# Graph layer kernel on one core: the second kind's tiles one lot earlier, and mask and maximum in one operation

## The reference, cut to what matters

```
h = relu(layernorm(x))
feat = concat(h[src], h[dst])
e_f  = relu(feat @ W_kind + b_kind)            # kind by the edge's number: 128 hh, 640 oo, 7680 ho
logit = e_f @ W_a + b_a
m = segment_max(logit, dst);  ex = exp(logit - m[dst])
alpha = ex / segment_sum(ex, dst)[dst]
z = segment_sum(alpha * h[src], dst)
x = x + relu(concat(h, z) @ (W_hn for nodes 0..63, W_on for 64..255) + b)
h = relu(layernorm(x));   W = zeros(1024, 1024); W[src, dst] += edge_weight
out = x + h @ W.T + bias
```

## Time and profile before

| | |
|---|---|
| median of 3 runs | 334.21 us (333.5 to 334.31) |
| the profiled execution's own time | 336.71 us |
| its span | 334.9 us |
| PE busy | 307.4 us (92%) |
| DVE busy | 255.0 us (76%) |
| ACT busy | 176.8 us (53%) |
| POOL busy | 159.2 us (48%) |
| DMA moved | 122.06 MB, mean 364 GB/s |
| granted TensorE clock | 0.99 of full |

### The profile page before, as it was taken

How to read it: one execution, slowest core, us unless ns; L and a number is a source line. 1 busy time by engine, 2 the same in 40 slices (tenths; PEclk the granted TensorE clock), 3 DMA queues, 4 the chain that set the end, 5 groups by cost and what they waited for, 6 DMA issues and landing times.

```text
span 334.9 us, 4146 instructions
## 1 busy us (share of the span) xinstructions
PE 307.4 (92%) x1363; PEld 195.8 (58%) x1363; DVE 255.0 (76%) x433; ACT 176.8 (53%) x437; POOL 159.2 (48%) x148
## 2 busy tenths in 40 slices
PE   0899999999999899999999999959998998889995
PEld 0687688745657466556666665645733554533533
DVE  4645527465999998998688888599897969996244
ACT  3865342371467663878356566466534847652102
POOL 3030057306877778788458887567777300000000
PEclk9999999999999999999999999979999999999997
DMA  7999979999999999999999999999999999999003
GB/s 247 409 410 410 363 247 297 373 415 339 352 394 410 410 409 409 410 407 412 415 410 410 409 411 411 414 410 409 410 408 412 406 410 406 405 408 350 17 0 125
DMA packets 34425, 122.06 MB, mean 364 GB/s; under 512 B 4058, under 2 KB 4570, under 8 KB 34404
## 3 DMA queue, kind: packets, MB, share of 16 engines
q0 software_dynamic: 19008, 69.21, 52.7%
q1 hardware_dynamic: 14004, 47.34, 36.7%
q10 hardware_dynamic: 1392, 5.24, 3.8%
HBM read 115.49 MB, written 6.29 MB: 364 GB/s over the span
## 4 chain that ended last, share of the span: by engine, by line
PE 29%; POOL 25%; DMA 25%; DVE 10%; issue 8%; ACT 2%; ACTq 0%; DVEq 0%
DMA Gq<-q_ho,ids 24%; POOL Gq L383 13%; PE psG L850 13%; POOL Gp L369 12%; PE psG L961 5%; DVE Gp L668 3%; PE psG L1063 2%; DVE Gp L672 2%; PE psG L1058 1%; PE psG L1014 1%; DMA xs<-x 1%; PE psW L1052 1%; PE psW L900 1%; ACT h L404 1%; DVE Wl L621 1%
## 5 line engine op out<-in xcount | busy, mean ns | idle before, releaser
L668 DVE TENSOR_TENSOR Gp<-Gp,Gq 128x1024 f32<-128x1024 f32 x65 | 79.4, 1221 | 26.2 <-DMA Gq<-q_ho,ids 24.1
L383 POOL DMA_INDIRECT Gq<-q_ho,ids x60 | 74.0, 1233 | 45.4 <-DVE Gp L668 16.1
L369 POOL DMA_INDIRECT Gp<-p_ho,ids x60 | 67.8, 1129 | 44.3 <-DMA p_ho<-T 24.4
L992 PE MATMUL psG<-W,hT 128*128 128x512 f32 x192 | 85.3, 594 | 0.0
L672 DVE SCALAR_TENSOR_TENSOR Gp<-Gp,wa 128x1024 f32<-128x1024 f32 x65 | 79.0, 1216 | 0.3
L478 ACT ACTIVATE RW<-ohs,ewh 128x256 fp32r<-128x256 f32 x66 | 33.2, 504 | 58.6 <-DVE ohs L659 54.3
L992 PEld LDWEIGHTS psG<-W,hT 128*128 128x128 f32 x192 | 35.6, 191 | 39.3 <-issue 38.9
L900 PE MATMUL psW<-RW,ohd 128*128 128x256 f32 x264 | 44.7, 291 | 0.4
L900 PE MATMUL psA<-RL,ohd 128*128 128x256 f32 x240 | 37.4, 299 | 8.1 <-ACT RL L488 7.4
L900 PEld LDWEIGHTS psA<-RL,ohd 128*128 128x128 f32 x240 | 31.7, 195 | 14.0 <-ACT RL L488 13.5
L900 PEld LDWEIGHTS psW<-RW,ohd 128*128 128x128 f32 x264 | 36.3, 189 | 4.1 <-issue 2.9
(11 more groups left out here) (174 smaller groups left out, 356.9 us busy)
## 6 DMA issues: line engine op xcount, KB each, us to landing
W<-weights SPq DMA_DIRECT2D x63, 512.0 KB, 7.4
Gp<-weights SPq DMA_DIRECT2D x8, 512.0 KB, 9.8
Gq<-weights SPq DMA_DIRECT2D x4, 512.0 KB, 12.6
pre_f<-weights SPq DMA_DIRECT2D x3, 512.0 KB, 7.3
xs<-x SPq DMA_DIRECT2D x2, 512.0 KB, 3.9
h_rows<-h ACTq DMA_DIRECT2D x1, 1024.0 KB, 6.7
pre_l<-weights SPq DMA_DIRECT2D x2, 512.0 KB, 7.0
p_ho<-T ACTq DMA_DIRECT2D x2, 512.0 KB, 5.0
```

The costliest lines, as they stand in the source:

```text
L369: nc.gpsimd.indirect_dma_start(out=Gp[:, i % NP, :], out_offset=None, in_=p_oo if t <= OO_TILES else p_ho, in_offset=bass.IndirectOffsetOn ...
L383: nc.gpsimd.indirect_dma_start(out=Gq[:, i % NQ, :], out_offset=None, in_=q_oo if t <= OO_TILES else q_ho, in_offset=bass.IndirectOffsetOn ...
L668: nc.vector.tensor_tensor(Gp[:, i % NP, :], Gp[:, i % NP, :], Gq[:, i % NQ, :], ALU.add).then_inc(s_sum, 1)
L992: last = nc.tensor.matmul(psG[:, 2 * t + half, :], hT[:, k, t * P:(t + 1) * P], W[:, s, half * HALF:(half + 1) * HALF], start=u != 1 and k ...
```

## The change

It sets BEFORE_OO to 48. Lot 17 becomes tiles 1, 2, 3, lot 18 tiles 4, 5, lot 19 tiles 54 to 56, and lots 20 to 23 stay as they are; LAST_OO becomes 18. `few_max` so runs after lot 19 and `few_sums` after lot 20. In `few_max`, the addition of the mask and the maximum become one instruction for each half of the destinations, the kind that `exp_in` uses at L753.

```diff
-BEFORE_OO = 51
+BEFORE_OO = 48
...
                 dve.wait_ge(s_Lfew, 2)
                 chain(nc.vector.tensor_tensor(L_few[:, :, :, :], L_few[:, :, :, :], inv_few[:, :, :, :], ALU.mult))
-                chain(nc.vector.tensor_tensor(L_few[:, :, :, :], L_few[:, :, :, :], off_few[:, :, :, :], ALU.add))
                 for c in range(NT):
-                    last = mark(nc.vector.tensor_reduce(mx[:, 0, c:c + 1], L_few[:, :, c, :], AX.XY, ALU.max))
+                    last = mark(nc.vector.tensor_tensor_reduce(out=L_few[:, :, c, :], in0=L_few[:, :, c, :],
+                                                               in1=off_few[:, :, c, :], scale=1.0, scalar=NEG, op0=ALU.add,
+                                                               op1=ALU.max, accum_out=mx[:, 0, c:c + 1]))
```

## The result

The changed kernel takes 332.73 us (median of 22 executions, 330.38 upward), the kernel before 334.31 (22 executions, 332.66 upward). The ratio is 0.9943, 95% interval 0.992 to 0.9965: 1.9 us less, between 1.2 and 2.7. The forecast was 331.3 with 2.95 us less. So the direction and the full range, 330.2 to 333.2, held, and the gain was a third smaller than forecast. The narrower range that the prediction gave its main case, 330.6 to 332.1, was missed, and the time is near the 332.3 of the rival "PE holds the end". The profiled execution took 332.81, its span is 331.0. The medians here are over all executions, while every ratio leaves out those that were disturbed, whatever the kernel.

A forecast was written before the change was run, and what follows sets the result against it. DVE was taken to wait for gathers up to 276.5, then to bound the end without a gap. Moving 3.91 us away, less 0.96 returned to landings, gives 2.95: 334.21 - 2.95 = 331.3 us, range 330.2 to 333.2.

The forecast's parts named there:

- main case: The forecast itself, last tile placed 2.95 us earlier: 331.3 us, own range 330.6 to 332.1, chance 0.6.
- PE holds the end: Rival: lot 20's late placing pushes PE, ACT still hands tiles over singly; gain 1.9 us, 332.3 us, chance 0.16.
- The two stages: DVE waits about 1 us per total for gathers up to 276.5, then works without a gap to the last logit.
- few_max in its new place: Behind total 56, 2.9 us instead of 3.91; total 57 is 1.8 late, 58 0.9 late, 59 on time.
- The landings: Gathers 60 and 61 land at 282.1 and 285.1, so DVE gives back 0.96 of 3.91 us, gaining 2.95.
- the step that failed: PE from lot 20 is shifted 0.9, reaches lot 21 at 290.2, places ready tiles faster, and ends at 297.3 or sooner.
- this sign of being wrong: Listed sign in the changed profile that would refute the forecast: no PE waits after 290, yet a late end.
- ACT and the second kind's copy: ACT's wait for few_max moves ahead of lot 21's weights instead of lot 22's; it costs nothing on this path.
- The tables: POOL's gather of position 48 waits for the q_oo store, landing at 214.3 before its issue at 215.79; no cost.
- Late gathers: Rival: weight loads get ahead of gather 60, 1.3 us each; two give nearly all back, 333.9 us, chance 0.12.
- slower: Rival: lot 20's 0.9 us delay on PE is not paid back and moves every later step; 335.1 to 336.1, chance 0.06.

The follow-up runs named there:

- the third one: Third profile of the changed kernel, unaltered, from a later measurement on another chip: ratio 0.9863 to the kernel before, 331.32 us.
- the first profile: Profile of the changed kernel from its first measurement: profiled execution 332.81 us, median 332.73 us, ratio 0.9943 to the kernel before.
- one lot more: Changed kernel with BEFORE_OO 45 instead of 48, one more lot earlier, mask and maximum fused: ratio 0.9914 to the kernel before, 332.72 us.
- the lots alone: Changed kernel with BEFORE_OO still 48 but the mask and maximum of few_max unfused: ratio 0.9946 to the kernel before, 333.67 us.
- less PE: Changed kernel with four of the six matmul calls of job 29 left out on PE: ratio 0.9853 to the kernel before, 331.9 us.

## Why the prediction was right, and where it was off

**The two stages** were read rightly. Work on DVE was paid from idle time before total 59 and reached the end behind it: `few_max`, made shorter in its old place, took its 1.23 off that stage.

**few_max in its new place**: 2.9 forecast, 2.7 measured, since a fused instruction takes 0.69 rather than the 0.78 that I worked out from the earlier trace rows. Total 59 was not late.

**The landings**: total 60 waits 1.00 where 0.7 was forecast, total 61 waits for nothing where 0.2 was. The stage on DVE is 18.85 against 18.54. That close match is of one profile: in the third one neither total waits for its gather, and the stage takes 17.76.

**PE** is the step that failed. The prediction said that from the placing of lot 20 to that of lot 21 all of PE's work is only shifted, which gave 290.2 - 278.2 = 12.0. It took 290.12 - 276.25 = 13.87. The 1.9 more are the lower clock: 0.6 in the placing (2.93 instead of 2.33) and 1.45 in four products (3.33 instead of 1.88), less what overlaps. The durations of the earlier trace rows came from an execution in which the clock was whole there, and I took them as fixed. The rest of that step held: ready tiles are placed in 1.58 instead of 2.33. At the full clock PE's way of 18.55 from 276.25 would have ended at 294.8, and DVE's side, 2.23 behind the last logit, at 295.8. So DVE would have held the end by 1.0, where the forecast had both together at 297.3, and the clock put PE 1.0 behind DVE instead. The prediction had named this sign of being wrong: PE has no waits after 290 and yet ends late.

**The rival "PE holds the end"** gave 1.9 us of gain, which is what was measured. Its reason was another: it had ACT handing tiles over one by one, and the trace shows them ready. In the first profile PE holds the end through the clock. So the forecast was right in its direction and in DVE's part, and it is luck that this rival's number is the measured one.

**ACT and the second kind's copy** I gave no cost to. In the profiles without that long wait this is right. But the prediction didn't look at how much room `few_max` had behind the copy of L_few, and that room went from 7.8 to 4.6 us.

**The tables**: in the changed kernel the gather of position 48 waits for a buffer as before, not for the store of q_oo. With one lot more POOL does wait for that store, 11.72 us, and DVE's totals come no later for it.

**Late gathers and slower** didn't come out as mechanisms. What the runs can't settle is why the same change is worth 0.57%, nothing and 1.4% in three measurements (0.9943, 0.9994, 0.9863, where the last two are of two chips and have intervals of half a per cent either way). Total 59 starts between 273.1 and 276.6 where DVE has the same work ahead of it, and I have no cause for that beyond the gathers that it waits for.

## What to carry to other kernels

Moving work out of a gapless last stage into one that waits for transfers gives its whole length only until the next engine is reached. Before counting on that, sum the next engine's work between its waits at both clock levels: a wait that seems to cost nothing may be what covers a slower stretch. And for a step moved earlier, measure the room to what it reads, not only the idle time around it.

## What the runs showed of the hardware that I hadn't expected

An addition with a running maximum over 128x512 f32 from SBUF takes 0.69 us on DVE, as long as the plain addition of that size (L730, 0.69), plus 0.08 for reading the accumulator, most of which overlaps: two follow each other at 0.62. The mask added to the maximum costs next to nothing over the reduction alone, which took 0.68 for each half.

TensorE's granted clock fell to 1.2 GHz between 275 and 276.4 us in some executions of a kernel and not in others (two of three profiles of the changed kernel). In all four profiles where it fell, PE waited 1.34 to 1.50 us for a one-hot; with the lots alone the clock fell in that wait, in the other three at or in the next one, of 1.31 or 1.32 for ACT. With the wait for ACT alone (before 1.32, one lot more 1.31, less PE 1.31) it stayed at 2.4. It also stayed there in the profiles with spare products of 0.25 us each in these waits, but not only in those, so that the products kept it up isn't shown. The Trainium skill (TensorE: Matmul & The Clock Gate, Part 1: The HAM clock gate) says that the clock is set by how busy the engine has been recently. These waits agree with that.
